# GpSimd order in the joint mixture program: small powers placed between transfers, the last two parts' scatters placed ahead of part 4's gathers

## The reference, cut to what matters

```python
x = x + 0.5 * _L0_ffn_ref(_layernorm(x), ...)      # 1
x = x + _L0_attn_ref(_layernorm(x), ...)           # 2
x = x + 0.5 * _L0_ffn_ref(_layernorm(x), ...)      # 3: gelu mixture, layer norm of its result
x = x + 0.5 * _L1_ffn_ref(_layernorm(x), ...)      # 4: swiglu mixture
x = x + _L1_attn_ref(_layernorm(x), ...)           # 5
x = x + 0.5 * _L1_ffn_ref(_layernorm(x), ...)      # 6
...
# _L1_ffn_ref: probs of x @ wg.T, top 2 renormalised, then
h1 = jnp.einsum('th,eih->tei', x, w1)
h3 = jnp.einsum('th,eih->tei', x, w3)
y = jnp.einsum('tei,ehi->teh', jax.nn.silu(h1) * h3, w2)
out = jnp.einsum('te,teh->th', expert_w, y)
```

## Time and profile before

| what | us |
|---|---|
| median of 3 runs without the profiler | 1375.79 |
| lowest and highest of them | 1371.82, 1377.14 |
| time of the profiled execution | 1379.39 |
| its span, first to last instruction | 1377.6 |

### The profile page before, as it was taken

One profiled execution on the slowest core, in us unless ns is written; L12 is line 12 of the kernel. 1 busy time (PEld: TensorE's weight loads), 2 busy tenths in 40 slices (PEclk: granted clock), 3 DMA queues, 4 the chain that ended last, 5 costly groups with the idle time before them and its releaser, 6 DMA issues. The chain is left out here.

```text
span 1377.6 us, 28236 instructions
## 1 busy us (share of the span) xinstructions
PE 1024.3 (74%) x6835; PEld 859.0 (62%) x6836; DVE 767.7 (56%) x2839; ACT 559.8 (41%) x1653; POOL 824.5 (60%) x802
## 2 busy tenths in 40 slices
PE   2599988627647799978679397199879974688981
PEld 2589988623347799977678387134343444688881
DVE  4433325358674344574447344469977977365542
ACT  1346656537514466754233033252255131223341
POOL 3668672741037676886877877364726644887665
PEclk9999999858968799998879799599999995799996
DMA  8848786400004566764566386000000000677884
GB/s 236 285 166 258 241 261 216 142 16 0 0 30 152 171 227 231 223 214 139 187 209 220 103 281 209 17 0 0 1 0 0 0 0 20 203 232 253 267 259 128
DMA packets 198793, 199.71 MB, mean 145 GB/s; under 512 B 22213, under 2 KB 140311, under 8 KB 198679
## 3 DMA queue, kind: packets, MB, share of 16 engines
q1 hardware_dynamic: 123138, 136.22, 29.1%
q0 software_dynamic: 16384, 33.59, 8.4%
q10 hardware_dynamic: 59156, 28.57, 7.4%
HBM read 52.44 MB, written 49.02 MB: 74 GB/s over the span
## 5 line engine op out<-in xcount | busy, mean ns | idle before, releaser
L611 PE MATMUL gelu_hb<-gelu_xsT,gelu_weights 128*128 128x128 f32 x2208 | 309.5, 286 | 6.8 <-issue 6.3
L611 PEld LDWEIGHTS gelu_hb<-gelu_xsT,gelu_weights 128*128 128x128 f32 x2208 | 284.9, 202 | 7.9 <-issue 6.9
L708 ACT ACTIVATE gelu_hid<-gelu_hb,gelu_weights 128x128 f32<-128x128 f32 x736 | 209.8, 371 | 133.0 <-PE gelu_hb L611 116.7
L1190 POOL DMA_INDIRECT slots_x<-gelu_xn,gelu_index x176 | 173.5, 986 | 102.3 <-DVE gelu_index L921 51.7
L622 PE MATMUL gelu_ob<-w,gelu_hid 128*128 x1472 | 200.4, 281 | 2.3 <-DVE gelu_ys L961 2.2
L622 PEld LDWEIGHTS gelu_ob<-w,gelu_hid 128*128 128x128 f32 x1472 | 185.2, 198 | 2.9 <-issue 2.9
L961 DVE TENSOR_TENSOR gelu_ys<-gelu_ob,bias 128x128 f32<-128x128 f32 x184 | 51.4, 291 | 216.7 <-PE gelu_ob L622 203.6
L602 PE MATMUL gelu_turn<-ident,gelu_xs 128*128 128x128 f32 x276 | 59.1, 298 | 76.0 <-DMA gelu_xs<-slots_x 69.1
L1850 POOL TENSOR_TENSOR rwkv_tw<-rwkv_tw,rwkv_qr 128x512 f32<-128x512 f32 x64 | 79.5, 1273 | 52.8 <-DVE rwkv_tw L1809 43.9
L611 PE MATMUL swiglu_hb<-swiglu_xsT,swiglu_weights 128*128 128x128 f32 x736 | 101.0, 282 | 0.4 <-DMA swiglu_weights<-s 0.4
L701 ACT COPY gelu_xsT<-gelu_turn 128x256 f32<-128x256 f32 x138 | 51.8, 375 | 121.1 <-PE gelu_turn L602 120.9
(11 more groups left out here) (375 smaller groups left out, 2043.7 us busy)
## 6 DMA issues: line engine op xcount, KB each, us to landing
gelu_weights<-w SPq DMA_DIRECT2D x184, 258.0 KB
gelu_weights<-s SPq DMA_DIRECT2D x92, 256.0 KB
swiglu_weights<-s SPq DMA_DIRECT2D x92, 256.0 KB
gelu_xs<-slots_x SPq DMA_DIRECT2D x69, 256.0 KB
slots_y<-gelu_ys ACTq DMA_DIRECT2D x138, 128.0 KB
swiglu_xs<-slots_x SPq DMA_DIRECT2D x23, 256.0 KB
slots_y<-swiglu_ys ACTq DMA_DIRECT2D x46, 128.0 KB
slots_x<-zeros SPq DMA_DIRECT2D x2, 1984.0 KB, 12.5
```

The lines of the kernel that those rows point to most:

```text
L611: last = pe.matmul(hb[j][:, c * P:(c + 1) * P], weights[:, j, c * P:(c + 1) * P], xsT[j // SET][:, j % SET, :], start=True, stop=True)
L708: last = act.activation(hid[:, j % RING, c * P:(c + 1) * P], hb[j][:, c * P:(c + 1) * P], ACT.Gelu, bias=weights[:, j, FF + c:FF + c + 1])
L1190: pool.indirect_dma_start(slots_x[:, :], bass.IndirectOffsetOnAxis(index[p][:, k, g:g + 1], 0), tokens[p][:, g, :], None).then_inc(sent[p] ...
```

## The change

Three tables and GpSimd's list are changed; no operation is added to or taken from the computation.

- GpSimd's list: `send(4, range(0, 4))` becomes `final_power(1, 2)`, `send(4, range(0, 2))`, and `final_power(2, 0)` follows it. `gate_power(5)` moves behind `fetch(3, 0)`. `fetch(3, 1)` is split by choice with `final_power(3, 0)` between, and `power(6)` comes before `final_power(3, 1)`. `power(7)`, `send(6)`, `gate_power(6)`, `send(7)`, `gate_power(7)` come before `fetch(4, 0)` and `fetch(4, 1)`.
- VectorE: `finish(3, 0)` and `stats(6)` move from iterations 30 and 31 to 29, `normalise(6)` from 31 to 30, and the further routing steps of parts 6 and 7 one iteration earlier or to an earlier slot. `gates(5)` moves from 28 to 35, `combine(4, ...)` from 33 and 34 to 39.
- TensorE and ScalarE: the steps of parts 6 and 7 one iteration earlier; `scale_lower(4, ...)` from 33 and 34 to 38.

```diff
@@ TensorE's table
-                                           32: {0: at(turn_tokens, 6, 0), 1: at(turn_tokens, 6, 1), 2: at(logits, 6, 0) + at(logits, 6, 1)},
-                                           33: {1: at(count_tokens, 6)},
...
+                                           31: {0: at(turn_tokens, 6, 0), 1: at(turn_tokens, 6, 1), 2: at(logits, 6, 0) + at(logits, 6, 1)},
+                                           32: {1: at(count_tokens, 6)},
...
@@ GpSimd's list
                 fetch(2, 0)
-                send(4, range(0, 4))
                 final_power(1, 2)
+                send(4, range(0, 2))
                 final_power(2, 0)
-                send(4, range(4, 6))
+                send(4, range(2, 6))
                 power(5)
...
                 send(5, range(4, 12))
-                gate_power(5)
                 await_sets(TILE0[4] // SET)
                 fetch(3, 0)
-                fetch(3, 1)
+                gate_power(5)
+                fetch(3, 1, choices=[0])
                 final_power(3, 0)
+                fetch(3, 1, choices=[1])
+                power(6)
                 final_power(3, 1)
-                power(6)
                 for p in (4, 5):
                     pool.wait_ge(sent[p], SENT[p])
-                await_sets(-(-TILE0[5] // SET))
-                fetch(4, 0)
                 power(7)
-                fetch(4, 1)
                 send(6)
                 gate_power(6)
                 send(7)
                 gate_power(7)
+                await_sets(-(-TILE0[5] // SET))
+                fetch(4, 0)
+                fetch(4, 1)
```

More of the change, by code:

```diff
@@ L683, in _ @@
                                            22: {0: at(logits, 5, 0) + at(logits, 5, 1) + at(logits, 5, 2), 3: at(count_tokens, 5)},
-                                           32: {0: at(turn_tokens, 6, 0), 1: at(turn_tokens, 6, 1), 2: at(logits, 6, 0) + at(logits, 6, 1)},
-                                           33: {1: at(count_tokens, 6)},
-                                           34: {1: at(turn_tokens, 7, 0), 2: at(logits, 7, 0)},
-                                           35: {1: at(count_tokens, 7)}}}[kinds]
+                                           31: {0: at(turn_tokens, 6, 0), 1: at(turn_tokens, 6, 1), 2: at(logits, 6, 0) + at(logits, 6, 1)},
+                                           32: {1: at(count_tokens, 6)},
+                                           33: {1: at(turn_tokens, 7, 0), 2: at(logits, 7, 0)},
+                                           34: {1: at(count_tokens, 7)}}}[kinds]
             run(pe, body, beside,
@@ L785, in _ @@
                                            30: {0: at(scale_lower, 3, 1)},
-                                           32: {0: at(copy_tokens, 6, 0), 1: at(copy_tokens, 6, 1)},
-                                           33: {0: at(scale_lower, 4, 0)},
-                                           34: {1: at(copy_tokens, 7, 0), 2: at(scale_lower, 4, 1)},
+                                           31: {0: at(copy_tokens, 6, 0), 1: at(copy_tokens, 6, 1)},
+                                           33: {1: at(copy_tokens, 7, 0)},
+                                           38: {1: at(scale_lower, 4, 0), 3: at(scale_lower, 4, 1)},
                                            40: {1: at(scale_lower, 5, 0)},
@@ L1109, in _ @@
                                            25: {2: at(finish, 2, 1)},
-                                           28: {2: at(gates, 5)},
-                                           29: {0: at(combine, 3, 0) + at(norm, 3, 0)},
-                                           30: {1: at(combine, 3, 1) + at(norm, 3, 1), 3: at(finish, 3, 0)},
-                                           31: {0: at(stats, 6), 1: at(finish, 3, 1), 3: at(normalise, 6)},
-                                           32: {1: at(stats, 7), 3: at(route, 6)},
-                                           33: {1: at(normalise, 7), 2: at(places, 6), 3: at(combine, 4, 0)},
-                                           34: {0: at(table, 6), 2: at(combine, 4, 1), 3: at(route, 7)},
-                                           35: {2: at(places, 7)},
-                                           36: {0: at(table, 7)},
+                                           29: {0: at(combine, 3, 0) + at(norm, 3, 0), 2: at(finish, 3, 0), 3: at(stats, 6)},
+                                           30: {1: at(combine, 3, 1) + at(norm, 3, 1), 3: at(normalise, 6)},
+                                           31: {1: at(finish, 3, 1), 2: at(stats, 7), 3: at(route, 6)},
+                                           32: {1: at(normalise, 7), 2: at(places, 6)},
+                                           33: {0: at(table, 6), 3: at(route, 7)},
+                                           34: {2: at(places, 7)},
+                                           35: {0: at(table, 7), 3: at(gates, 5)},
                                            37: {3: at(gates, 6)},
+                                           39: {0: at(combine, 4, 0), 2: at(combine, 4, 1)},
                                            38: {2: at(gates, 7)},
```

## The result

| | before | after |
|---|---|---|
| median, us (18 runs each, same chip) | 1374.66 | 1377.91 |
| lowest and highest, us | 1368.03, 1378.11 | 1374.15, 1384.52 |
| ratio after / before, 95% interval | | 1.0034 (1.0021 to 1.0047) |
| span of the profiled execution, us | 1377.6 | 1375.4 |

Predicted were 1378.8 us, a rise of 3.0; measured were 1377.91, a rise of 3.2 between these medians, and of 4.7 (2.9 to 6.5) by the ratio. It is smaller than the 0.5% that the prediction took as the limit; with 18 runs of each, the interval of the ratio still lies clear of 1. The two spans go the other way, by 2.2 us: one execution of each kernel can't show 3 us at the end of the program. So I compare a stretch inside the layer, which I call **the stage**: from the end of part 5's last scatter to the end of the last gather. In before part 5's last scatter, which the rows ahead don't show, is

A forecast was written before the change was run, and what follows sets the result against it. GpSimd's list was taken as the bound from 689 us on: part 6's `index` at 741.9 plus 132.6 us of work gives 874.5 against 871.5, 3.0 later; 1375.8 + 3.0 = 1378.8 us, range 1370 to 1386.

The forecast's parts named there:

- Part one: Final powers placed between part 4's scatters on GpSimd: worth 0, bounds a gain of 6.2 us and a loss of 0.3.
- Landing of part 3's last gather: From that gather's issue on GpSimd to its use in `combine(3, 1)` on VectorE: 2.6 us, rows giving 1.6 to 3.4.
- `index` of part 6: VectorE's routing result that part 6's scatters wait for: ready at 741.9 us instead of 748.2.
- or 3 longer: Upper bound on the 17.6 us from `normalise(6)` to part 6's `index`: it might take 3 us more.
- GpSimd idle in all: GpSimd's waits from part 5's scatters to the last gather: 21 us, against 18.1 before.
- Work behind the `index`: Scatters and gate powers of parts 6 and 7, then gathers of parts 4 to 7, on GpSimd: 132.6 us.
- TensorE resumes at 769.7: TensorE gets part 6's scattered rows 13.7 us earlier than 783.43; its wait shrinks from 17.9 to about 9 us.
- ScalarE's wait of 9 us: At `scale_lower(4, 1)`, iteration 38: ScalarE waits 9 us for part 4's late gather, landing at 800.9.
- The products' end: TensorE's last products of the layer end at about 858 us instead of 854.
- No new wait: GpSimd, from part 6's `index` to its last gather, was taken to get no new wait for stored results.
- Rival B: Late gathers hold the product loop, products end past 860, end moves 4 to 6 us more: 1384; chance 0.22.
- Rival A: TensorE is the bound, so its 13.7 us carry through to the end: 1362.1 us; chance 0.12.

The follow-up runs named there:

- the four corners: Part 4's gathers ahead of or behind part 6's scatters, part 6 routed as before or earlier: ratios 1 (before), 1.0063 (gathers behind), 0.9961 (routed earlier), 1.0034 (both).
- all four kernels of one chip: The changed kernel with two, three or four of part 4's gather blocks ahead of part 6's scatters, or eight pauses there: ratios to before 0.9959, 0.9938, 0.9961, 1.0055.

## Why the prediction was right, point by point

- **What bounds the layer: right.** The stage shows GpSimd's list as the bound; pauses behind the `index` cost 9.8 us of stage for 8.65, and products that got their rows 12.4 us earlier brought no gain. The Trainium skill, "Perfetto Trace Analysis", section "Optimization Strategy", says to find the gaps of the engine that one optimises for, within the regime of interest, since the most contended engine can change over time. The trace agrees. Over the whole span TensorE leads (74% busy), and its longest gap here shrank from 17.92 to 11.33 us without a gain; within the stage of before GpSimd leads, busy for 132.6 of 182.4 us against TensorE's 126.2.
- **Part one, 0: right.** That edit alone has a ratio of 0.9998, and `normalise(5)` starts at 623.24 against 623.13.
- **Landing of part 3's last gather, 2.6 us: 2.3.** From 713.90 + 0.95 to 717.17. The estimate of 2.2 us from the Trainium skill, "DMA: Bandwidth & Descriptors", section "Anatomy of one DMA — SWDGE (gpsimd) path", was nearer than my middle row: by that page's fixed cost the trace agrees here to 0.1 us, while the last gather was used 1.65 us behind the end of its issue, below the fixed cost. `combine(3, 1)` starts 30.1 us behind part 5's scatters; predicted 719.7 - 689.2 = 30.5. `normalise(6)` starts at 34.8; predicted 35.1.
- **`index` of part 6: 1.3 us later than predicted.** 741.06 - 687.03 = 54.0 us behind part 5's scatters against 741.9 - 689.2 = 52.7. From `normalise(6)` to the `index` it took 740.89 + 0.17 - 721.78 = 19.3 us instead of 17.6: `finish(3, 1)` now lies inside, and TensorE comes out of a wait of 4.3 us just before it, at 721.44; both stand in the prediction's bound "or 3 longer". How the 1.7 us divide between them was not tried.
- **GpSimd idle in all: 22.8 us against 21.0**, most of the difference being that later `index`.
- **Work behind the `index`: 131.4 us (741.06 to 872.50) against 132.6.** Scatters and gate powers took 777.77 + 1.05 - 741.36 = 37.5 (predicted 37.8), the gathers 872.50 - 778.82 = 93.7 (94.7). This error of 1.2 and the one of 1.3 above cancel, so that the sum of 3.0 comes so near to the 3.1 measured is luck; its terms are each right to about 1 us.
- **TensorE resumes at 769.7**, 80.5 behind part 5's scatters: measured 81.9, with the wait 11.3 instead of some 9. **ScalarE's wait of 9 us** was 7.55, at the place named. **The products' end** was put at 858, 168.8 behind; it was 171.0. These are off by 1.4 to 2.3 us and cost nothing, since GpSimd isn't waiting for them.
- **"No new wait" behind the `index`: right, with little to spare.** The trace puts the gather at 861.46, the last of part 6, down to a store of results, but its idle time of 0.30 us is the usual gap. Part 7's first gather could start at 862.44, so the last results were there about 1 us before it, an estimate. Rival B's mark, products that end past 860, was just reached: 171.0 us behind part 5's scatters is 689.2 + 171.0 = 860.2 in before's clock. Its waits on ScalarE and VectorE are there too; what did not follow is the wait of GpSimd and with it the 4 to 6 us.
- **Rival A** is refuted here; its premise, that the products are the bound, holds on the slower chip. The prediction did not reckon with two chips that differ in what bounds the layer.

## What to carry to other kernels

Treat the idle time of an in-order engine ahead of a dependency as a budget: bring the dependency forward, then fill what is left of the wait with work that must be done anyway, block by block, until the engine arrives just as the dependency does. The change did the first half (worth 7 us) and undid the second (cost 10). When two halves of an edit can have opposite signs, run the four corners before judging either.

## What was not expected of the hardware

One chip ran the same kernel 16% slower (1592 against 1372 to 1375 us) with GpSimd's instructions at their usual length, the DMA engines busy for the same time (401 us in the largest queue), TensorE busy 10% longer, and another engine as the bound of this layer; a gain measured on one chip (0.9938) and on the other (0.9919) can thus be the same size for different reasons. A landing of an indirect gather, from the end of its issue to its use, was 1.65 us (872.50 to 874.15) to 2.3 us. Eight pauses in a row take 8.65 us, 1.08 each, where most single ones take 1.00 to 1.05. And what stays open: why all four kernels of one chip take 2.4 to 3.4 us more against before's launch times than their stage says, and what makes the slow chip slow.
